# A long convolution with its operands swapped, in one stage of a twelve-layer decoder kernel

## The reference

```python
def s4d(x, log_dt, A_re, A_im, C_re, C_im, D_skip):
    ...
    K = 2.0 * jnp.einsum('dn,dnl->dl', dC, powers).real
    n = 2 * L
    Kf = jnp.fft.rfft(K, n=n, axis=-1)
    xf = jnp.fft.rfft(x, n=n, axis=1)
    y = jnp.fft.irfft(xf * Kf.T[None], n=n, axis=1)[:, :L]
    return y + x * D_skip
...
    x = layernorm(x_text, g_norm_in, b_norm_in)
    scale_in, shift_in = jnp.split(c_t @ W_film_in + b_film_in, 2, axis=-1)
    x = x * (1.0 + mod_gate * scale_in) + mod_gate * shift_in
    y = s4d(x, log_dt, A_re, A_im, C_re, C_im, D_skip)
    scale_out, shift_out = jnp.split(c_t @ W_film_out + b_film_out, 2, axis=-1)
    y = y * (1.0 + mod_gate * scale_out) + mod_gate * shift_out
    xt = x_text + y
    h = layernorm(xt, g_ffn, b_ffn)
    h = jax.nn.gelu(h @ W1 + b1, approximate=False) @ W2 + b2
    xt = xt + h
    return layernorm(xt, g_norm_out, b_norm_out)
```

## Time and profile before

| | us |
|---|---|
| median of 3 runs | 4582.13 |
| lowest and highest run | 4579.23, 4591.21 |
| the profiled execution | 4580.66 |
| its span in the profile | 4578.9 |
| mean granted TensorE clock, of full speed | 0.922 |
| TensorE, VectorE, ScalarE, GpSimd busy | 3831.4, 2800.7, 2112.3, 1172.6 |

### The profile page before, as it was taken

How to read it: one execution, slowest core, us unless ns; L and a number is a source line. 1 busy time by engine, 2 the same in 40 slices (tenths; PEclk the granted TensorE clock), 3 DMA queues, 4 the chain that set the end, 5 groups by cost and what they waited for, 6 DMA issues and landing times. The chain is left out here.

```text
span 4578.9 us, 84527 instructions
## 1 busy us (share of the span) xinstructions
PE 3831.4 (84%) x33378; PEld 2565.5 (56%) x33378; DVE 2800.7 (61%) x7503; ACT 2112.3 (46%) x3569; POOL 1172.6 (26%) x819
## 2 busy tenths in 40 slices
PE   0688888888899879998999996654779999598999
PEld 0466666566556556664555554433547776465665
DVE  9577777666899756666565554985242222476555
ACT  4466666544333225555555544441364444354332
POOL 3444444222344311002455452321110000010000
PEclk9999999999999859999999998776689999798999
DMA  2222222100000001000000000003300000000000
GB/s 93 45 49 48 47 47 48 22 1 1 1 1 1 1 12 41 2 1 1 2 2 2 2 2 1 15 21 114 121 1 1 1 1 1 28 2 2 1 10 10
DMA packets 59436, 91.90 MB, mean 20 GB/s; under 512 B 16306, under 2 KB 42628, under 8 KB 57796
## 3 DMA queue, kind: packets, MB, share of 16 engines
q1 hardware_dynamic: 54916, 80.88, 7.5%
q10 hardware_dynamic: 4128, 5.64, 0.4%
HBM read 42.30 MB, written 10.62 MB: 12 GB/s over the span
## 5 line engine op out<-in xcount | busy, mean ns | idle before, releaser
L853 PE MATMUL banks<-XT,weight_region 128*128 128x512 f32 x1696 | 781.2, 599 | 2.3 <-DVE T L1229 2.3
L875 PEld LDWEIGHTS banks<-weight_region,HT 128*128 128x128 f32 x4672 | 560.5, 192 | 151.5 <-issue 91.7
L1252 DVE SCALAR_TENSOR_TENSOR x_res<-banks,WT,x_res 128x128 f32<-128x128 f32 x1056 | 297.1, 343 | 489.4 <-PE banks L875 449.6
L875 PE MATMUL banks<-weight_region,HT 128*128 128x128 f32 x4672 | 570.1, 276 | 21.6 <-DVE HT L1240 15.2
L853 PEld LDWEIGHTS banks<-XT,weight_region 128*128 128x128 f32 x1696 | 305.8, 193 | 288.5 <-issue 283.2
L1005 ACT ACTIVATE HT<-banks,weight_region 128x512 f32<-128x512 f32 x256 | 173.1, 687 | 240.0 <-PE banks L853 233.7
L1068 POOL TENSOR_TENSOR FNM<-FNM,FRS 128x8 f32<-128x8 f32 x16 | 4.6, 286 | 1014.4 <-ACT FRS L964 1014.4
L458 DVE TENSOR_REDUCE MX<-banks 128x8 f32<-128x1152 f32 x128 | 173.1, 1352 | 115.8 <-PE banks L275 113.8
L384 ACT COPY PT<-banks 128x384 f32<-128x384 f32 x384 | 171.4, 480 | 131.5 <-PE banks L285 129.7
L1643 ACT COPY PT<-banks 77x512 f32<-77x512 f32 x256 | 142.8, 582 | 186.9 <-PE banks L1565 186.8
L1096 POOL TENSOR_TENSOR T<-T,T 128x512 f32<-128x512 f32 x128 | 162.6, 1272 | 210.6 <-ACT T L1028 208.1
(11 more groups left out here) (472 smaller groups left out, 8589.7 us busy)
## 6 DMA issues: line engine op xcount, KB each, us to landing
FL<-RAW SPq DMA_DIRECT2D x512, 64.0 KB, 2.3
T<-s4d_k_dram SPq DMA_DIRECT2D x8, 1024.0 KB, 5.8
weight_region<-in_l_ffn__w_dram SPq DMA_DIRECT2D x2, 2048.0 KB, 8.6
film_dram<-F SPq DMA_DIRECT2D x8, 512.0 KB, 2.9
weight_region<-in_l_ffn__w_dram ACTq DMA_DIRECT2D x2, 2048.0 KB
FO<-film_dram SPq DMA_DIRECT2D x8, 512.0 KB, 4.1
x_res<-in_x_dram SPq DMA_DIRECT2D x1, 2048.0 KB
weight_region<-in_l_ffn__w_dram SPq DMA_DIRECT2D x2, 1024.0 KB, 10.6
```

Of the source, the lines that this page charges most:

```text
L853: nc.tensor.matmul(PS[:, q % 4, :], w, xt, start=True, stop=True).then_inc(s.h_ps, 1)
L875: ins = nc.tensor.matmul(PS[:, 4 + u % 2, b * P:(b + 1) * P], HT[:, u % 2, j, b * P:(b + 1) * P], w2[j], start=j == 0, stop=j == len(w2) - 1)
L1252: ins = nc.vector.scalar_tensor_tensor(R[:, t, :], PS[:, 4 + u % 2, b * P:(b + 1) * P], WT[:, t, e:e + 1], R[:, t, :], ALU.mult, ALU.add)
```

## The change

Four things change together.

In `s4d_conv` the operands of the convolution are swapped. UR's 32 columns of one feature (a column each 512 bytes) are stationary, the Toeplitz block streams with its 128 columns, and four features are worked on in the four quarters of 32 output partitions of a bank. The result of a chunk (YT: partition is quarter and sequence, column is group of four and token) is copied by ScalarE to SBUF, turned back by four transposes, and copied by VectorE. T has three buffers instead of two, U is loaded in four parts, and the flips start at the first.

Y isn't stored: VectorE writes it to the last 4096 columns of the weight region (`E.y_all`), and `l2_close` reads it there. `y_dram` and its loads are gone.

The stage's weight loads move from ScalarE's queue to SyncE's, behind the T loads, and are only those of `l2_ffw` (1414 columns a partition, 8 loads, 0.7 MB).

The expert weights of `l2_ffn` (5 loads, 4.3 MB) are issued by SyncE in `l2_close`, one behind each of its first five FO loads; those of `l3_attn` and `l3_xattn` by SyncE in `l2_ffn`.

```diff
-def s4d_conv(nc, E, k_dram, u_dram, y_dram, prefetch):
+def s4d_conv(nc, E, k_dram, u_dram, prefetch):
...
-        U = sb("U", [P, B_ALL, P]); Y = sb("Y", [P, B_ALL, P]); T = sb("T", [P, 2, DCH, P]); UR = sb("UR", [P, B_ALL, P])
+        U = sb("U", [P, B_ALL, P]); UR = sb("UR", [P, B_ALL, P]); T = sb("T", [P, 3, DCH, P]); YT = sb("YT", [P, 2, 4, P])
...
-                sp.dma_start(U[:], u_dram).then_inc(s.u_ld, 16)
+                def toeplitz(c):
+                    if c >= 3:
+                        sp.wait_ge(s.yt_ps, c - 2)
+                    src = k_dram[c * DCH:(c + 1) * DCH, :]
+                    sp.dma_start(T[:, c % 3], bass.AP(tensor=src.tensor, offset=src.offset + 1, ap=[[1, P], [2 * P, DCH], [1, P]])).then_inc(t_ld[c % 3], 16)
+
+                for q in range(NU):
+                    sp.dma_start(U[:, q * BU:(q + 1) * BU], u_dram[:, q * BU:(q + 1) * BU]).then_inc(u_ld[q], 16)
                 for c in range(NCH):
...
-                sp.wait_ge(s.y, NCH)
-                sp.dma_start(y_dram, Y[:]).then_inc(s.y_st, 16)
-                sp.wait_ge(s.y_st, 16)
+                    toeplitz(c)
+                for dst, src in prefetch:
+                    sp.dma_start(dst, src).then_inc(s.w_ld, 16)
+                sp.wait_ge(s.w_ld, 16 * len(prefetch))
+
+            @block.tensor
+            def _(pe):
+                def back(c):
+                    pe.wait_ge(s.yt, c + 1)
+                    if c >= 4:
+                        pe.wait_ge(s.y, c - 3)
+                    pe_transpose4(nc, [YT[:, c % 2, q, :] for q in range(4)], y_bank(c), E.ident).then_inc(s.y_ps, 1)
...
+                for c in range(NCH):
+                    pe.wait_ge(t_ld[c % 3], 16 * (c // 3 + 1))
+                    if c >= 4:
+                        pe.wait_ge(s.yt, c - 3)
+                    for q in range(4):
+                        for i in range(4):
+                            ins = nc.tensor.matmul(yt_bank(c)[32 * i:32 * (i + 1), q * P:(q + 1) * P], UR[:, :, c * DCH + 4 * q + i], T[:, c % 3, 4 * q + i, :],
+                                                   start=True, stop=True)
+                    ins.then_inc(s.yt_ps, 1)
+                    if c:
+                        back(c - 1)
+                back(NCH - 1)
 
             @block.scalar
             def _(act):
-                for dst, src in prefetch:
-                    act.dma_start(dst, src).then_inc(s.w_ld, 16)
-                act.wait_ge(s.w_ld, 16 * len(prefetch))
...
-                    for i in range(DCH):
-                        ins = nc.tensor.matmul(PS[:, c, i * B_ALL:(i + 1) * B_ALL], T[:, c % 2, i, :], UR[:, :, c * DCH + i], start=True, stop=True)
-                    ins.then_inc(s.y_ps, 1)
+                    act.wait_ge(s.yt_ps, c + 1)
+                    if c >= 2:
+                        act.wait_ge(s.y_ps, c - 1)
+                    nc.scalar.copy(YT[:, c % 2].rearrange("p q j -> p (q j)"), yt_bank(c)).then_inc(s.yt, 1)
...
-                    nc.vector.tensor_copy(Y[:, :, c * DCH:(c + 1) * DCH], PS[:, c, :].rearrange("p (i b) -> p b i", i=DCH)).then_inc(s.y, 1)
...
+                    nc.vector.tensor_copy(E.y_all[:, :, c * DCH:(c + 1) * DCH], y_bank(c).rearrange("p (i b) -> p b i", i=DCH)).then_inc(s.y, 1)
...
@@ l2_close @@
-                    sp.dma_start(Y[:, g % 3], of(y_dram, g)).then_inc(loads[g % 3], 16)
                     sp.dma_start(FO[:, g % 3], of(fo_dram, g)).then_inc(loads[g % 3], 16)
+                    for dst, src in prefetch[g::NG]:
+                        sp.dma_start(dst, src).then_inc(s.w_ld, 16)
+                sp.wait_ge(s.w_ld, 16 * len(prefetch))
...
-                    nc.vector.scalar_tensor_tensor(x, FO[:, g % 3, :, 0:P], 1.0, Y[:, g % 3], ALU.add, ALU.mult).then_inc(s.m1, 1)
+                    nc.vector.scalar_tensor_tensor(x, FO[:, g % 3, :, 0:P], 1.0, of(E.y_all, g), ALU.add, ALU.mult).then_inc(s.m1, 1)
...
@@ decoder @@
-        s4d_conv(nc, E, k_dram, u_dram, y_dram, place(["l2_ffw", "l2_ffn", "l3_attn", "l3_xattn"], 0))
-        run("l2_ffw", l2_close, y_dram=y_dram, fo_dram=fo_dram)
-        run("l2_ffn", l2_ffn)
+        E.y_all = region[:, REGION - B_ALL * P:REGION].rearrange("p (b d) -> p b d", b=B_ALL)
+        close, experts = place(["l2_ffw"], 0), place(["l2_ffn"], FFW, REGION - B_ALL * P)
+        s4d_conv(nc, E, k_dram, u_dram, close)
+        run("l2_ffw", l2_close, fo_dram=fo_dram, prefetch=experts)
+        run("l2_ffn", l2_ffn, prefetch=place(["l3_attn", "l3_xattn"], REGION - B_ALL * P))
```

More of the change, by code:

```diff
@@ L2598, in s4d_conv, with flip_bank, yt_bank, y_bank @@
     NCH = P // DCH
-    with sublayer(nc, "u_ld t_ld0 t_ld1 ur_ps ur y_ps y y_st w_ld") as (s, ctx):
+    NU = 4
+    with sublayer(nc, "u0 u1 u2 u3 t0 t1 t2 ur_ps ur yt_ps yt y_ps y w_ld") as (s, ctx):
         sb = E.scratch(ctx)
-        U = sb("U", [P, B_ALL, P]); Y = sb("Y", [P, B_ALL, P]); T = sb("T", [P, 2, DCH, P]); UR = sb("UR", [P, B_ALL, P])
-        t_ld = [s.t_ld0, s.t_ld1]
+        U = sb("U", [P, B_ALL, P]); UR = sb("UR", [P, B_ALL, P]); T = sb("T", [P, 3, DCH, P]); YT = sb("YT", [P, 2, 4, P])
+        u_ld = (s.u0, s.u1, s.u2, s.u3)
+        t_ld = (s.t0, s.t1, s.t2)
+        BU = B_ALL // NU
+        def flip_bank(c):
+            return PS[:, c % 4, :]
+        def yt_bank(c):
+            return PS[:, c % 4, :]
+        def y_bank(c):
+            return PS[:, 4 + c % 4, :]
         with nc.Block() as block:
@@ new lines, in _ @@
+                for c in range(NCH):
+                    toeplitz(c)
[9 more added lines that the diff above has]
+                    pe_transpose4(nc, [YT[:, c % 2, q, :] for q in range(4)], y_bank(c), E.ident).then_inc(s.y_ps, 1)
+                for c in range(8):
+                    if c % 2 == 0:
+                        pe.wait_ge(u_ld[c // 2], 16)
+                    if c >= 4:
+                        pe.wait_ge(s.ur, c - 3)
+                    nc.tensor.matmul(flip_bank(c), E.flip, U[:, 4 * c:4 * c + 4, :].rearrange("p b d -> p (b d)"), start=True, stop=True).then_inc(s.ur_ps, 1)
+                pe.wait_ge(s.ur, 8)
+                for c in range(NCH):
+                    pe.wait_ge(t_ld[c % 3], 16 * (c // 3 + 1))
+                    if c >= 4:
+                        pe.wait_ge(s.yt, c - 3)
[7 more added lines that the diff above has]
+                back(NCH - 1)
@@ L2638, in _, with l2_close @@
                     dve.wait_ge(s.ur_ps, c + 1)
-                    nc.vector.tensor_copy(UR[:, 4 * c:4 * c + 4, :].rearrange("p b d -> p (b d)"), PS[:, c, :]).then_inc(s.ur, 1)
+                    nc.vector.tensor_copy(UR[:, 4 * c:4 * c + 4, :].rearrange("p b d -> p (b d)"), flip_bank(c)).then_inc(s.ur, 1)
                 for c in range(NCH):
                     dve.wait_ge(s.y_ps, c + 1)
-                    nc.vector.tensor_copy(Y[:, :, c * DCH:(c + 1) * DCH], PS[:, c, :].rearrange("p (i b) -> p b i", i=DCH)).then_inc(s.y, 1)
-def l2_close(nc, E, y_dram, fo_dram):
+                    nc.vector.tensor_copy(E.y_all[:, :, c * DCH:(c + 1) * DCH], y_bank(c).rearrange("p (i b) -> p b i", i=DCH)).then_inc(s.y, 1)
+def l2_close(nc, E, fo_dram, prefetch):
     W, PS = E.w, E.ps
@@ L2751, in film_rest @@
                 def film_rest(g):
-                    pool.wait_ge(loads[g % 3], 32 * (g // 3 + 1))
+                    pool.wait_ge(loads[g % 3], 16 * (g // 3 + 1))
                     f = FO[:, g % 3, :, P:2 * P]
@@ L2787, in modulate @@
                     x = R[:, g % 4]
-                    dve.wait_ge(loads[g % 3], 32 * (g // 3 + 1))
+                    dve.wait_ge(loads[g % 3], 16 * (g // 3 + 1))
                     if g >= 4:
                         dve.wait_ge(s.g2, g - 3)
-                    nc.vector.scalar_tensor_tensor(x, FO[:, g % 3, :, 0:P], 1.0, Y[:, g % 3], ALU.add, ALU.mult).then_inc(s.m1, 1)
+                    nc.vector.scalar_tensor_tensor(x, FO[:, g % 3, :, 0:P], 1.0, of(E.y_all, g), ALU.add, ALU.mult).then_inc(s.m1, 1)
                     dve.wait_ge(s.m1, g + 1)
@@ L2931 @@
 RESID = 7812
+FFW = 1414
 def load_block(nc, todo):
```

11 lines of the change are left out of this document (2 added, 9 removed).

## The result

| | before | after |
|---|---|---|
| median of the runs, us | 4584.33 (4, among them the three of the first table) | 4541.09 (4) |
| lowest and highest | 4579.23, 4591.21 | 4538.87, 4542.06 |
| the profiled execution, and its span | 4580.66, 4578.9 | 4538.87, 4537.1 |
| from the first load of U to the first load of the next stage | 88.53 | 42.32 |
| everything ahead of that | 3168.24 | 3172.43 |

The ratio of after to before is 0.9904, with a 95% interval of 0.9887 to 0.9921: a gain of 36 to 52 us.

The account below looks back on a forecast made before the run. The convolution stage was taken as four pieces in series: loads 25.5 us, TensorE's convolution 55.1, last copy and store 7.0, border 0.9. Stage gain 46.7 plus 0.4 made 47.1 us, so 4535 us, range 4522 to 4556.

Parts of the forecast that it names:

- The quarters: Convolution matmuls on TensorE: four quarter matmuls cost 0.43 us, so a chunk of 16 costs 1.72 us instead of 6.88.
- one change of form: TensorE's switch between quarter matmuls and transposes: about 0.15 us each, 16 of them 2.4 us, inside 2.9 us per chunk.
- B: Rival at UR's strided stationary read: 0.215 us per load, 8.1 us a chunk, total 4574; 10% for the upper end.
- C: Rival at the convolution's quarters: they don't overlap, each pass costs 0.423 us, 118 us in all, total 4627; 3%.
- The pace: Loads of T in the convolution: queued behind each other with three buffers, 3.6 us per chunk, ends 3.4 and 3.9.
- Rival A: Loads of T don't queue up: blocks come 5.8 us apart, 17.6 us more, total 4553; 9%.
- The last block: Last load of T: there 35.9 us into the stage, from 1.3 + 5.3 + 8 x 3.6 + 0.5.
- The head: Start of the stage: first bytes after about 1.3 us, U's 2.1 MB in 5.3, first quarter in at about 3.1.
- an empty queue because UR came late: T loads after the flips: no gap expected; with all flips at the lower clock, a gap of 3.6 us.
- The tail: Behind the last T block: quarters, ScalarE copy, transposes, VectorE copy and steps, together 5.0 us, then a border of 0.9.
- 0.4 us of earlier FO: Start of l2_close: without the Y load ahead of FO, 0.4 us less of issue before the first modulate.
- Case D: TensorE clock in l2_close: it wanders, about 1.6 us a group over eight groups, up to 12 us either way.

Follow-up runs that it names:

- x_no_reload: Changed kernel without five of the eight T loads, chunks 3 to 7 reusing the first three blocks; stage 33.40 us, median 4533.27 us.
- x_two_queues: Changed kernel with every second block of T issued from ScalarE's queue instead of SyncE's; stage 46.17 us, ratio to before 0.9916.
- x_weights_head: Changed kernel with 5.0 MB of l2_ffw and expert weights issued by ScalarE at the convolution's head; stage 56.39 us, ratio to before 0.9939.
- v_preload_2: Second set of the changed kernel with two T blocks loaded a stage early, four buffers for the other six; stage 35.10 us, ratio to before 0.9875.
- x_two_buffers: Changed kernel with two buffers of T instead of three; stage 47.69 us, ratio to before 0.9906.
- before_again: The kernel before, unedited, profiled a second time; stage 88.64 us, starting at 3173.60, median 4586.03 us.
- v_preload_contig: Changed kernel with two T blocks loaded a stage early and UR laid out contiguously by feature; stage 34.86 us, ratio to before 0.9897.
- x_keep_only: Changed kernel with the old convolution (T stationary, two buffers, U in one load), Y kept and weights moved; stage 70.88 us, ratio to before 0.9971.
- a_again: The changed kernel once more, unedited, beside the kernel before; stage 42.28 us, ratio to before 0.9898.

## Why the prediction was right, point by point

**4535 was predicted, 4541 measured (4539 in the second set).** By spans, the profile gave 41.8 us: 46.2 in the stage, -4.2 ahead of it, -0.2 behind it. The prediction said 46.7 in the stage, nothing ahead and 0.4 behind. Over all medians (before 4584.9 in 39 runs, after 4541.1 in 8) the gain is 43.8.

**The quarters.** Predicted 1.72 us a chunk at the lower clock with no more than a contiguous load; measured 1.94 to the start of the transposes. With the 0.15 predicted for one change of form, under 0.1 is left for the stride. Cycle at the upper clock 1.75 us (x_no_reload); at the lower one 2.9 predicted, and 3.06 us busy out of each 3.5 seen. The Trainium skill (TensorEngine Tiling (Array Packing), Key Properties) says that a change of mode drains TensorE. Whatever that costs is inside these cycles, as read from the cross attention's rows, and adds nothing to the stage; no run measured it alone. Rivals B (0.215 us a load, 6.9 a chunk) and C (118 us) are refuted.

**The pace.** Predicted 3.6 us a block; measured 3.51 to 3.60 between the last five. It is the transfers that set it, since TensorE without them needs half (x_no_reload) and a second queue gives no more (x_two_queues). Rival A (5.8) is refuted; even with two buffers the blocks came 4.0 to 4.3 us apart on average.

**The last block.** Predicted to be there 35.9 us into the stage, in fact 38.1 (3210.56). Two terms were too small. The head: U's first quarter was in at 3.9 us (3176.37) instead of 3.1, and the third block at 18.9 (3191.33) instead of 17.9. And the even pace of the sum failed at one step: between the third and the fourth block's chunk lie 5.06 us, 1.5 more than the pace. It is not what I had feared, an empty queue because UR came late. UR was late by 0.5 only (13.6, predicted 13.1), and the engines moved 292 GB/s in those 5.06 us (the stretches above), 1.48 MB for one block of 1.05. In x_weights_head, where the reload was issued with a whole block still ahead of it, the same step took 5.08 us at 292 GB/s. So the bytes came, but part of them were those of the block behind. Up to the fourth landing, 7.0 MB were moved for the 6.3 of U and four blocks. At the third landing it was 5.5 for 5.2, so part of the head's 1.0 us may be the same thing. The sum should have had one term more, about 0.4 MB or 1.5 us, for a block whose landing is counted when its last part is in, while the next one's bytes flow beside it. It isn't that the fourth load is the first into a used buffer. In v_preload_2 the fourth load of T waits for no chunk, and it lands as late, 23.9 us into the stage (3195.23), with as many bytes moved (a stretch, columns as above):

```profile
3171.36:3195.23 23.87, 17.77 (x193) 10.72 (x193) 8.29 (x12) 3.49 (x5) 0.00 (x0) 0.81 1.09 293
```

In the changed kernel it is 24.0 us and 7.0 MB too. Why it falls on the fourth block wasn't settled.

**The tail.** Predicted 5.0 and a border of 0.9; in fact 3.4 (3210.56 to 3213.91) and 0.8. TensorE was at the upper clock again in the last chunk, 1.2 us for its quarters where 1.7 was taken. That was not sure to happen: in x_two_buffers and x_two_queues the last chunk ran at the lower clock and the tail with the border took 5.5 us, near the 5.9 predicted. The two misses, +2.2 and -1.7, nearly cancel, so the 41.8 against the 42.3 is partly luck. The stage's own weights cost nothing: they landed in time for the border.

**Behind the stage.** The predicted 0.4 us of earlier FO did not come: the first modulate is 5.1 us behind the border, not 4.1, for a reason that the runs don't show (3.5 to 5.2 us in the kernels with the same order of loads). The later groups hid the expert loads, as predicted: from the first load of `l2_close` to TensorE's first instruction in `l2_ffn` are 134.9 us in before, 135.2 in after. Case D, the clock in `l2_close`, stayed away: the hidden layer's passes have a median of 834 ns before and 824 after.

**What the prediction didn't see** is how the parts depend on each other. It added them up once and was right in the sum, but the share of each (24.0 for the swap alone, 14.1 for the weights once the swap is in) came only from the runs. (A slip in its working changed nothing: the parts of its upper bound add up to 4554, not 4552.)

**Still open.** Why unchanged code ahead of the stage takes between 3163.6 and 3175.1 us. Part of it lies in `l1_xattn` (TensorE's first instruction there to its first in the next stage 238.7 us in before, 245.5 in before_again, 240.4 in after, 245.5 in v_preload_contig), so it is not tied to either kernel. All loads of T here read runs of 512 bytes; whether another layout of the filters in DRAM moves faster wasn't tried. Loading U already reversed, which would do without the flips and their 9 us, wasn't tried.

## What to carry to other kernels

Where a stationary block is used for few columns, make the narrow operand the stationary one and use the column quarters: the same products went from 6.88 to 1.94 us a chunk here, at the same clock (3.06 with the turning back). Then look for what the slow engine had been hiding, since that is where the next third of the gain lies: the weight loads at the stage's head cost 7.5 us before (5.6 MB) and 14.1 after (5.0 MB). Once transfers are the pace, buffers count until the queue never runs dry (the third one was worth 4.1 us). A second queue didn't help here; moving bytes out of the stage did (3.55 us a block).

## What the runs showed of the hardware

- Weight loads that are busy for the whole of a stretch did not keep the clock up: in before the granted clock was 0.50 through the full 128x128 loads with 32 streamed columns. In x_keep_only, where they follow right behind the flips, it held 1.00 for the first chunk and fell during the second, with TensorE busy for 6.00 of 6.00 us. In after it held 1.00 for the first three chunks of quarters and fell to 0.50 at the fourth (0.59 over 3196.39 to 3199.99), after TensorE had been idle for 3.2 us. In v_preload_2, with waits of 1.1 to 1.7 us, it kept 1.00 to the end of the stage.
- The same code does not get the same clock each time. In a_again it fell one chunk sooner than in after, behind a wait of 1.5 us (0.53 over 3192.57 to 3197.27), and was back at 1.00 in the seventh chunk. The stage was 42.28 us all the same, since the loads are the pace:

```profile
3192.57 1.92 PE L2654 MATMUL banks<-T,UR 128*32 128x128 f32 x32 [1.54 <-DMA T<-s4d_k_dram]
...
3208.02 1.22 PE L2654 MATMUL banks<-T,UR 128*32 128x128 f32 x32 [0.90 <-DMA T<-s4d_k_dram]
```

- A stationary block of 32 columns read at a stride of 512 bytes: 138 ns for the shortest load against 106 contiguous, and 0.14 to 0.19 us for 16 matmuls at the upper clock.
- Loads of 512-byte runs, queued behind each other, move 291 GB/s from one queue (279 to 295 over single blocks), and 286 from two queues. A load behind others takes about 10 us to land, but the next one follows 3.5 us later.
- A load's landing says little about the bytes moved by then: 1.48 MB went by between two landings of 1.05 MB.
- The same code took up to 11 us more or less ahead of this stage from one execution to another. A gain of 5 to 10 us was safe only in the stage's own time.
